# Mixture-of-experts stage: result buffers in threes, shared results added in groups of 3, 3, 2 and 2, gathers issued two experts further ahead

## What is computed

```
x = x + xattn(layernorm(x), k, bias, ctx, ctx)      # a long convolution over products
x = x + ffn(layernorm(x), ...)                       # mixture of experts

scores = softmax(xf @ gate_w.T);  topk_w, topk_idx = top_k(scores, 6)      # 64 experts
# each expert takes its first 128 tokens, in order of token number
gu  = gx @ gate_up_proj[e];  g, u = split(gu)                              # 512 -> 2 * 192
eo  = (silu(g) * u) @ down_proj[e] * weight                                # 192 -> 512
routed = scatter_add(eo, tokens of e)
shared = silu(xf @ shared_gate_w.T) * (xf @ shared_up_w.T) @ shared_down_w.T   # 512 -> 384 -> 512
return x + routed + shared
```

## Time and profile before

| | |
|---|---|
| median of three runs | 1161.11 us |
| profiled execution, whole time | 1163.35 us |
| its span | 1161.5 us |
| PE busy | 1086.0 us, 94% of the span |
| PE weight loads | 851.7 us, 73% |
| DVE busy | 828.7 us, 71% |
| POOL busy | 736.9 us, 63% |
| ACT busy | 527.3 us, 45% |
| DMA | 217.08 MB, mean 187 GB/s |
| mean granted clock of PE | 0.975 |

### The profile page before, as it was taken

How to read it: one execution, slowest core, us unless ns; L and a number is a source line. 1 busy time by engine, 2 the same in 40 slices (tenths; PEclk the granted TensorE clock), 3 DMA queues, 4 the chain that set the end, 5 groups by cost and what they waited for, 6 DMA issues and landing times. The chain is left out here.

```text
span 1161.5 us, 17623 instructions
## 1 busy us (share of the span) xinstructions
PE 1086.0 (94%) x5113; PEld 851.7 (73%) x5113; DVE 828.7 (71%) x1424; ACT 527.3 (45%) x958; POOL 736.9 (63%) x434
## 2 busy tenths in 40 slices
PE   3999999999999999999699999999999799999953
PEld 2778777787777777877599998777777567777632
DVE  3799999999999999998589963555655345655623
ACT  5565556555665556553422222444434334444411
POOL 6999999999999999993024223245345245445422
PEclk9999999999999999999899999999999889999977
DMA  6365554456445554452385445699999889999964
GB/s 188 97 189 159 165 146 135 146 158 166 129 135 157 165 148 134 144 151 73 109 269 154 129 127 153 197 286 284 294 289 280 222 255 289 291 280 282 284 166 52
DMA packets 92029, 217.08 MB, mean 187 GB/s; under 512 B 11239, under 2 KB 16167, under 8 KB 91856
## 3 DMA queue, kind: packets, MB, share of 16 engines
q1 hardware_dynamic: 75440, 177.75, 50.5%
q0 software_dynamic: 16544, 38.78, 15.8%
HBM read 164.82 MB, written 52.18 MB: 187 GB/s over the span
## 5 line engine op out<-in xcount | busy, mean ns | idle before, releaser
L1059 POOL TENSOR_TENSOR ring<-vT,pT 128x1024 f32<-128x1024 f32 x128 | 249.2, 1958 | 9.5 <-ACT vT L803 9.3
L445 PE MATMUL Y<-split,toep 128*128 128x512 f32 x576 | 238.2, 414 | 11.1 <-ACT toep L797 8.9
L1067 POOL TENSOR_TENSOR split<-ring,split 128x1024 fp32r<-128x1024 f32 x96 | 231.0, 2406 | 1.1 <-ACT split L809 1.1
L447 PE MATMUL Y<-split,toep 128*128 128x512 f32 x576 | 227.2, 394 | 0.0
L446 PE MATMUL Y<-split,toep 128*128 128x512 f32 x576 | 225.9, 392 | 0.0
L689 PE MATMUL Y<-ring,xT 128*128 128x384 f32 x512 | 194.3, 503 | 0.0
L1236 DVE TENSOR_TENSOR z<-Y,cT 128x1024 f32<-128x1024 f32 x128 | 157.0, 1226 | 26.6 <-PE Y L449 25.5
L1242 DVE TENSOR_REDUCE o<-z 128x128 f32<-128x1152 f32 x128 | 172.1, 1345 | 1.2
L445 PEld LDWEIGHTS Y<-split,toep 128*128 128x128 f32 x576 | 109.0, 189 | 31.2 <-issue 9.8
L809 ACT ACTIVATE split<-ring 128x1024 fp32r<-128x1024 f32 x96 | 100.8, 1050 | 58.2 <-POOL ring L1059 58.2
L447 PEld LDWEIGHTS Y<-split,toep 128*128 128x128 f32 x576 | 108.6, 189 | 24.4
(11 more groups left out here) (168 smaller groups left out, 1909.7 us busy)
## 6 DMA issues: line engine op xcount, KB each, us to landing
ring<-_L_ffn_gate_up_proj_dram SPq DMA_DIRECT2D x64, 768.0 KB
ring<-in_L_ffn_down_proj_dram SPq DMA_DIRECT2D x64, 384.0 KB
gr<-filters SPq DMA_DIRECT2D x32, 512.0 KB, 4.1
stage<-in_x_dram SPq DMA_DIRECT2D x32, 256.0 KB, 5.5
pT<-in_turned_dram SPq DMA_DIRECT2D x32, 256.0 KB, 4.1
cT<-in_turned_dram SPq DMA_DIRECT2D x32, 256.0 KB, 4.1
xr<-in_x_dram SPq DMA_DIRECT2D x32, 256.0 KB, 3.9
xn_rows<-xn SPq DMA_DIRECT2D x32, 256.0 KB, 2.9
```

What stands on the lines that cost most here:

```text
L445: pe.matmul(y, high, kv[:, s, 0, a, n], start=(a == 0), stop=False)
L447: last = pe.matmul(y, low, kv[:, s, 0, a, n], start=False, stop=(a == c))
L1059: pool.tensor_tensor(to.rearrange("p (b j i) -> p b j i", i=NH, j=NH), a, d, ALU.mult).then_inc(kvp_ready, 1)
L1067: pool.tensor_tensor(kv[:, s, 1, c, :], kvp[c], kv[:, s, 0, c, :].bitcast(F32), ALU.subtract).then_inc(kv_ready, 1)
```

## The change

The result buffers become three pairs: `NO` = 3, and the third pair lies in `pT`, which the third stage does not use otherwise. Every `eo[k % 2]` becomes `eo[k % NO]`, and the copies wait for the scatter of pair k - 3. (`eb`, the split result for PE, stays at two.)

`BATCH` = 5 gives way to `GROUPS` = (3, 6, 8, 10): the shared tiles are added three before pair 6, three before pair 15, two before pair 21 and two before pair 27. `shared_done` and ACT's wait for a free `y2` buffer follow the new groups.

The gathers of pair k are now those of experts 2k + 8 and 2k + 9 (for k = 0: 6 to 9), before the group of shared tiles and before the scatters of pair k.

```diff
--- before.py
+++ after.py
@@ -45,7 +45,7 @@
 LIST_AT = MOVE_AT + 3
 NB = MOVE_AT + 4
 NY2 = 6
-BATCH = 5
+GROUPS = (3, 6, 8, 10)
 EPS = 1e-5
 FLOOR = -87.3
 OTHER, MARK = 1.0, 2.0
@@ -54,6 +54,7 @@
 NW = 4
 NG = 8
 NY = 4
+NO = 3
 
 
 def build(nc, x, skip, ctx_in, k, gate_w, gate_up, down, sh_gate, sh_up, sh_down,
@@ -149,7 +150,8 @@
         firsts, both = w[:, 1, 0:CAP], w[0:E, 1, 0:2 * CAP]
         xg = [stage[:, g, :] for g in range(NG)]
         y2 = [sc_all[:, 8 * n:8 * n + 8, :].rearrange("p a e -> p (a e)") for n in range(4)] + [xr[:, n, :] for n in range(2)]
-        eo = [[y[:, 0, :], y[:, 1, :]], [w[:, 0, :], w[:, 1, :]]]
+        eo = [[y[:, 0, :], y[:, 1, :]], [w[:, 0, :], w[:, 1, :]],
+              [pT[:, n, :, :].rearrange("p c n -> p (c n)") for n in range(2)]]
 
         YY = [ps(f"Y{n}", 2) for n in range(2)]
         Y = [YY[n // 2][:, n % 2 * 512:(n % 2 + 1) * 512] for n in range(4)]
@@ -971,7 +973,7 @@
                     act.wait_ge(prob_out, B * 16)
                     act.wait_ge(y_ready, NB)
                 elif n >= NY2:
-                    act.wait_ge(y2_added, ((n - NY2) // BATCH + 1) * BATCH * 16)
+                    act.wait_ge(y2_added, min(g for g in GROUPS if g > n - NY2) * 16)
                 act.activation(y2[n % NY2], Y[2][:, :], ACT.Copy).then_inc(y2_ready, 1)
 
             b_evacuate_hid(NB - 1, 1)
@@ -1014,7 +1016,7 @@
                 act.wait_ge(eb_ready, k + 1)
                 if k > 1:
                     act.wait_ge(moved_ps, k - 1)
-                act.activation(eb[:, k % 2, 0, :], eo[k % 2][1], ACT.Copy).then_inc(eb_high, 1)
+                act.activation(eb[:, k % 2, 0, :], eo[k % NO][1], ACT.Copy).then_inc(eb_high, 1)
 
             def c_iteration(e):
                 if e % 2 and e > 1:
@@ -1109,7 +1111,8 @@
 
             def shared_done(k):
 
-                return sum(pieces(2 * n + 1)[1] == "out" for n in range(k + 1)) // BATCH * BATCH
+                done = sum(pieces(2 * n + 1)[1] == "out" for n in range(k + 1))
+                return max((g for g in GROUPS if g <= done), default=0)
 
             def add(k, a):
                 if a:
@@ -1125,7 +1128,7 @@
                     pool.wait_ge(y2_added, shared_done(k) * 16)
                 pool.sem_inc(pool_turn, 1)
                 pool.indirect_dma_start(out=out, out_offset=bass.IndirectOffsetOnAxis(ap=idx, axis=0),
-                                        in_=eo[k % 2][a], in_offset=None, bounds_check=T + CAP - 1, oob_is_err=False,
+                                        in_=eo[k % NO][a], in_offset=None, bounds_check=T + CAP - 1, oob_is_err=False,
                                         compute_op=ALU.add).then_inc(added[a], 16)
 
             def b_rows_low(t, s):
@@ -1156,27 +1159,19 @@
             def add_shared(last, k):
                 for a in range(2):
                     pool.wait_ge(added[a], k * 16)
-                for t in range(last + 1 - BATCH, last + 1):
+                for t in range(NB + shared_done(k - 1), last + 1):
                     pool.wait_ge(y2_ready, t - NB + 1)
                     pool.dma_start(rows(out[0:T, :], t), y2[(t - NB) % NY2], accum_op=ALU.add).then_inc(y2_added, 16)
 
             for s in range(2):
                 pool.wait_ge(y_out[s], NB // 2 * 16)
                 pool.wait_ge(x1_out[s], NT // 2 * 16)
-            fetched = NG - 2
             for k in range(E // 2):
+                for e in range(2 * k + NG if k else NG - 2, min(2 * k + NG + 2, E)):
+                    fetch(e)
                 t, part = pieces(2 * k + 1)
-                shared = part == "out" and (t - NB + 1) % BATCH == 0
-                upto = min(2 * k + NG, E)
-                for e in range(fetched, upto):
-                    fetch(e)
-                fetched = max(fetched, upto)
-                if shared:
+                if part == "out" and t - NB + 1 in GROUPS:
                     add_shared(t, k)
-                    upto = min(fetched + 2, E)
-                    for e in range(fetched, upto):
-                        fetch(e)
-                    fetched = upto
                 for a in range(2):
                     add(k, a)
             for a in range(2):
@@ -1554,25 +1549,25 @@
             def c_result_b(k):
                 e = 2 * k + 1
                 dve.wait_ge(c_down, e + 1)
-                if k < 2:
+                if k < NO:
                     dve.wait_ge(y_out[1], NB // 2 * 16)
                 else:
-                    dve.wait_ge(added[1], (k - 1) * 16)
-                dve.tensor_copy(eo[k % 2][1], DN[1][:, :]).then_inc(eb_ready, 1)
+                    dve.wait_ge(added[1], (k + 1 - NO) * 16)
+                dve.tensor_copy(eo[k % NO][1], DN[1][:, :]).then_inc(eb_ready, 1)
 
             def c_result_b_low(k):
                 dve.wait_ge(eb_high, k + 1)
-                dve.tensor_tensor(eb[:, k % 2, 1, :], eo[k % 2][1], eb[:, k % 2, 0, :].bitcast(F32), ALU.subtract).then_inc(eb_low, 1)
+                dve.tensor_tensor(eb[:, k % 2, 1, :], eo[k % NO][1], eb[:, k % 2, 0, :].bitcast(F32), ALU.subtract).then_inc(eb_low, 1)
 
             def c_result_a(k):
 
                 e = 2 * k
                 dve.wait_ge(moved_ps, k + 1)
-                if k < 2:
+                if k < NO:
                     dve.wait_ge(y_out[0], NB // 2 * 16)
                 else:
-                    dve.wait_ge(added[0], (k - 1) * 16)
-                dve.tensor_copy(eo[k % 2][0], ca[k % 2][:, :]).then_inc(ea_ready, 1)
+                    dve.wait_ge(added[0], (k + 1 - NO) * 16)
+                dve.tensor_copy(eo[k % NO][0], ca[k % 2][:, :]).then_inc(ea_ready, 1)
 
             def c_iteration(e):
                 k = e // 2
```

## The result

The changed kernel takes 1152.90 us, the median of 20 runs from 1144.85 to 1161.78. The kernel before, now also run 20 times, has 1158.17 us, from 1152.08 to 1162.35: the three runs that stood above were at the upper end of what it does. Their ratio is **0.9961, with an interval from 0.9945 to 0.9976**: faster by 5.3 us between the medians (4.5 by the ratio), where 18 us had been forecast. The profiled execution took 1151.69 us with a span of 1149.8, against 1163.35 and 1161.5: 11.7 us less.

A forecast was written before the change was run, and what follows sets the result against it. PE was taken to bound the experts stage except for two holes from late scatters. Scatter periods of 11.4 us plus four groups' holds gave a span 18.5 us shorter; taken from the median, 1143 us, range 1129 to 1158.

The forecast's parts named there:

- What bounds the kernel: Experts stage: PE sets the pace, 12.32 us a pair, except two holes from late scatters; the first costs 14.85 us.
- Slack of copies and gathers: Lateness of scatters borne before PE stalls: copies 19.4 us with three buffer pairs, gathers 16.7 us when fetched further ahead.
- The period of the chain: POOL issues a pair's scatters only after the previous pair's landed: 11.4 us a pair under load, bounds 10.5 and 12.8.
- light periods at the end: Last pairs, scatters alone on the queues: three periods of 7.88 us, after one half under load of 9.6.
- Rival E: Slower: loaded scatter period exceeds PE's pair, deciding at 12.3 us, so four drains add up; about 1167 us, chance 0.10.
- hold of a group: First tile's issue to next scatters: 3.5 us fixed plus 2.67 a tile; three 11.5 us, two 8.8, last group 10.9.
- The sum: Scatter times added from pair 5 at 806.63 to pair 31 at 1131.3, plus 11.7: span 1143.0 against 1161.5.
- tiles' starts: Each group's tiles start 10.9 us after the preceding scatters, a period less about 0.5 us.
- the base: Saving of 18.5 us within the profiled execution was taken from the runs' median of 1161.11, giving 1142.6, stated as 1143.
- rival C: Stall only moves: three tiles 14.6 us, period 11.7, PE waits for gathers at pair 21; 1150 to 1157, chance 0.18.
- PE's path: PE's progress without holes, 12.32 us a pair: pair 21's scatters at 1003.8, the chain 15.5 us late there.
- What would show it: Signs: clock 1.00 from 860 to 980 us, gather waits under 5 us, threes 11 to 12 us, pair 31 near 1131.

The follow-up runs named there:

- run 20: Not a label but part of "now also run 20 times": the kernel before, unchanged, median 1158.17 us, from 1152.08 to 1162.35.
- first two experiments: Kernel before with only the third pair of result buffers: 1156.93 us, ratio 0.998; with only the gathers two experts further ahead: 1155.83 us, ratio 0.9968.
- two groups of five: Changed kernel with shared tiles again added five and five; third buffer pair and earlier gathers stay: 1149.69 us, ratio 0.9929 to the kernel before.
- single tiles: Changed kernel with ten groups of one shared tile each, the first before pair 0: 1162.96 us, ratio 1.0037 to the kernel before.
- 1, 4 and 5: Changed kernel with groups of one, four and five shared tiles before pairs 0, 12 and 27: 1150.36 us, ratio 0.9916 to the kernel before.
- 1, 5 and 4: Changed kernel with groups of one, five and four shared tiles before pairs 0, 15 and 27: 1146.84 us, ratio 0.9901 to the kernel before.
- Without any group: Changed kernel without the adding DMAs of the ten late shared tiles and their waits, their result left out of the output: 1132.41 us, ratio 0.9772.
- the best: Lowest median of all: changed kernel with groups of one, five and four shared tiles before pairs 0, 15 and 27: 1146.84 us, ratio 0.9901.

## Why the prediction was wrong, point by point

**What bounds the kernel** was read rightly: holes made by late scatters, through the copy and through the gather. Each part alone removes just its own wait (first two experiments).

**Slack of copies and gathers** (19.4 and 16.7 us): it held. Scatters 15.5 us late (two groups of five, pair 12) make PE wait for nothing. In the changed kernel pair 15 comes at 951.64, 21.8 us after 944.71 - 14.85 = 929.86. That is 2.4 us over the first slack, and DVE's copy waits 2.06; it is 5.1 over the second, and PE waits 5.56:

```profile
964.67 1.08 PE L679 MATMUL TA<-sq,stage 128*128 128x128 f32 x4 [5.56 <-DMA stage<-xn_rows,idx_i]
```

**The period of the chain**, 11.4 us: between the groups it was (924.26 - 830.40)/8 = 11.7, (1008.08 - 951.64)/5 = 11.3 and (1085.61 - 1030.60)/5 = 11.0, single ones from 8.5 to 14.5. As a mean it was right. So were the light periods at the end (8.0 for 7.9). Rival E, which needed a period over 12.3, did not come about.

The places of the scatters, as forecast and as in the profile of the changed kernel:

| scatters of pair | 6 | 14 | 15 | 20 | 21 | 26 | 27 | 31 | span |
|---|---|---|---|---|---|---|---|---|---|
| forecast | 829.0 | 920.2 | 942.6 | 999.6 | 1019.3 | 1076.3 | 1098.1 | 1131.3 | 1143.0 |
| measured | 830.4 | 924.3 | 951.6 | 1008.1 | 1030.6 | 1085.6 | 1107.5 | 1139.6 | 1149.8 |

**The first step that failed is the hold of a group.** The sum split it into 3.5 us fixed, from the shortest landing of a gather, and 2.67 a tile, and took 11.5 us for three tiles and 8.8 for two. They were 12.50 and 15.60, 11.06 and 10.72. With the 6.4 + 2.3 n that the single tiles show, three cost 13.3 and two 11.0: 1.8 + 1.8 + 2.2 + 0.1 = 5.9 us more over the four groups, and the sum's span of 1143.0 becomes 1148.9, against 1149.8 measured. Term by term, in this one execution, the four holds were 7.2 us over their forecasts and the tiles' starts, 11.2 to 11.8 us after the scatters instead of 10.9, another 2.2; the loaded periods came to 0.1 more in all, the last periods and what follows them to 2.7 less. So part of the closeness of 1148.9 is errors that cancel. The bounds (10.1 to 14.6 and 6.7 to 10.9) held two of the four. The value in them was chosen by a row that was no nearer than others: the shortest landing of a gather says little of an adding transfer issued under load. It also hid what the change does to itself: at 6.4 us a drain, four groups instead of two put 12.8 us on the chain (10.5 in these two profiles, whose holds add up to 49.9 and 39.3). The chain, late from pair 6 on instead of from 12, regains only a part of that: 6.6 us are left at pair 27 (1107.52 for 1100.95 with two groups of five).

**The second is the base.** The sum was a difference within one execution, and 18.5 us were taken from the median. But the profiled execution of before was 5.2 us over the 20 runs' median, and that of after 1.2 under its own: 6.4 us of the 11.7 that the two profiles show are not between the kernels. The prediction's own absolute figure, 1143.0 + 1.85 = 1144.9, stands 8 us under the measured median, 5.9 of it by the holds. In which rows the old kernel's profiled execution lost its 5 us is not settled; its second hold of 21.95 us is the longest seen, but the four other kernels with five tiles there had 18.3, 20.2, 21.3 and 21.4.

**What happened is nearer to rival C**, the stall that only moves, than to the forecast. C had three tiles at 14.6 us and a period of 11.7, pair 21 over 20 us late, and PE waiting for gathers after pairs 15 and 21 and then at a low clock. The two threes had a mean of 14.05; pair 21 came at 1030.60, 26.8 us after the 1003.8 of PE's path; PE waited 5.56 and 2.53 us, with the granted clock at 0.91 and 0.96 in those windows. The median of 1152.9 lies in C's range, 1150 to 1157, which had a chance of 0.18. That it lies near C's middle is partly luck: C counted its losses from the same 18.5 us, too large by the base.

**What would show it**: the clock stayed at 1.00 to 940, not to 980 us; PE waited 8.1 us for gathers, not under 5; the threes took 12.5 and 15.6, not 11 to 12. Those three told of the same term. Pair 31 came at 1139.57 for 1131.

## What to carry to other kernels

Where transfers must follow each other because they add to the same rows, count each drain of that chain by itself: a group costs a fixed time that does not shrink with it, and cutting a batch into smaller ones shortens the longest hold while it lengthens the sum. Give the engines enough buffers and look-ahead to bear the longest hold, and then make the groups few, and one of them where the chain is idle anyway. That an earlier place helps was not shown: 1, 4 and 5 was no faster than 1, 5 and 4. And before a forecast of one per cent, ask whether the profiled execution is a typical one: here the runs of one kernel span 10 us and more.

## What the runs showed of the hardware

A 256 KB adding DMA from SBUF to DRAM, issued by GpSimd while weights stream, adds 2.3 us to a group's hold, and the group itself costs 6.4 us (from single tiles at 8.7 and fives at 17.8 us; more before pair 27). That fixed part is above the 2.0 us of fixed cost that the Trainium skill states for a DMA of this path (DMA: Bandwidth & Descriptors, "Anatomy of one DMA"); by that rule the sum would have been still lower, and the measurement decides.

Without any group five runs lie within 4 us; the kernels with groups spread over 5 to 17 us, except the best, whose five lie within 2. Whether it is the chain's lateness that spreads them was not tried.
